# Gated linear attention on one core: the sixteen state steps of a half as one scan along the free axis

## The reference

```python
def step(S, inp):
    qt, kt, vt, gt = inp
    S = S * jnp.exp(gt)[..., None] + kt[..., None] * vt[..., None, :]
    ot = jnp.einsum('bhk,bhkv->bhv', qt, S)
    return (S, ot)
S0 = jnp.zeros((b, h, dk, dv), q.dtype)
_, o = jax.lax.scan(step, S0, (qT, kT, vT, gT))
...
g = jax.nn.log_sigmoid(x @ Wgk1 @ Wgk2 + bgk2) / GLN
```

## Time and profile before

| what | value |
|---|---|
| median of 3 runs | 3053.11 us (3050.43 to 3057.81) |
| span of the profiled execution | 3058.2 us, first to last instruction |
| first stage, of that span | about 676 us |
| PE busy, whole span | 2879.5 us (94%) |
| DVE busy, whole span | 2283.9 us (75%) |
| ACT busy, whole span | 1938.1 us (63%) |

### The profile page before, as it was taken

How to read it: one execution, slowest core, us unless ns; L and a number is a source line. 1 busy time by engine, 2 the same in 40 slices (tenths; PEclk the granted TensorE clock), 3 DMA queues, 4 the chain that set the end, 5 groups by cost and what they waited for, 6 DMA issues and landing times. The chain is left out here.

```text
span 3058.2 us, 63018 instructions
## 1 busy us (share of the span) xinstructions
PE 2879.5 (94%) x22889; PEld 1806.1 (59%) x22890; DVE 2283.9 (75%) x4031; ACT 1938.1 (63%) x3559; POOL 688.5 (23%) x965
## 2 busy tenths in 40 slices
PE   5999999986999999999999999999888999999998
PEld 4777777774333333333333333337777888888886
DVE  5777777764999999999999999967785454545443
ACT  3666666661888888888888888875543333333332
POOL 2222222222000000000000000001103555555554
PEclk7899999986999999999999999998889999999999
DMA  1223323223222222222222222217642333333332
GB/s 45 87 98 107 111 101 105 100 84 117 68 74 65 83 72 72 67 67 65 73 72 69 66 64 72 73 39 212 213 146 51 50 50 50 49 51 49 50 50 42
DMA packets 170745, 243.05 MB, mean 79 GB/s; under 512 B 30920, under 2 KB 118240, under 8 KB 170512
## 3 DMA queue, kind: packets, MB, share of 16 engines
q1 hardware_dynamic: 121920, 170.57, 18.4%
q0 software_dynamic: 31152, 52.33, 8.9%
q10 hardware_dynamic: 17440, 16.98, 1.7%
HBM read 126.53 MB, written 111.21 MB: 78 GB/s over the span
## 5 line engine op out<-in xcount | busy, mean ns | idle before, releaser
L1030 DVE TENSOR_REDUCE b_mxq<-b_p_m 128x1 f32<-128x1024 f32 x1024 | 1220.6, 1222 | 76.2 <-PE b_p_m L1057 67.2
L964 ACT ACTIVATE b_probs<-b_p_e 128x512 f32<-128x512 f32 x2048 | 1105.4, 597 | 140.7 <-PE b_p_e L1110 40.1
L1057 PE MATMUL b_p_m<-b_kst,b_qst 64*128 64x512 f32 x1536 | 568.2, 449 | 0.8 <-DVE b_mxq L1030 0.8
L1110 PE MATMUL b_p_e<-b_qst,b_kst 64*128 64x512 f32 x1536 | 559.6, 444 | 0.2 <-ACT b_probs L964 0.2
L1082 PE MATMUL b_p_o<-b_probs,b_vst 128*32 128x256 f32 x6160 | 481.9, 390 | 0.5 <-ACT b_probs L964 0.4
L1110 PEld LDWEIGHTS b_p_e<-b_qst,b_kst 64*128 64x128 f32 x1536 | 236.4, 184 | 312.3 <-ACT b_probs L964 266.0
L1849 ACT ACTIVATE d_act<-d_p_up 128x512 f32<-128x512 f32 x136 | 81.2, 597 | 490.7 <-PE d_p_up L1922 490.7
L1082 PEld LDWEIGHTS b_p_o<-b_probs,b_vst 128*32 128x32 f32 x6160 | 126.3, 108 | 243.4 <-issue 133.4
L1818 POOL DMA_INDIRECT out_dram<-d_y,d_to x136 | 217.7, 1601 | 216.8 <-DVE d_y L1883 204.1
L1937 PE MATMUL d_p_y<-w2T,d_hT 128*128 x1096 | 259.1, 379 | 0.8 <-ACT d_hT L1843 0.8
L1865 DVE TENSOR_SCALAR d_xh<-d_p_x,d_ln 128x128 fp32r<-128x128 f32 x272 | 82.9, 346 | 233.5 <-PE d_p_x L1916 233.5
(11 more groups left out here) (319 smaller groups left out, 4628.5 us busy)
## 6 DMA issues: line engine op xcount, KB each, us to landing
b_qst<-qk_d SPq DMA_DIRECT2D x288, 64.0 KB
b_kst<-qk_d SPq DMA_DIRECT2D x288, 64.0 KB
qk_d<-a_hi SPq DMA_DIRECT2D x32, 512.0 KB, 2.8
qk_d<-a_lo SPq DMA_DIRECT2D x32, 512.0 KB, 3.8
v_d<-a_v_s SPq DMA_DIRECT2D x16, 1024.0 KB, 4.5
o_d<-b_oT POOLq DMA_DIRECT2D x63, 256.0 KB, 2.7
b_vst<-v_d SPq DMA_DIRECT2D x48, 256.0 KB
raw<-in_L_ffn_w_dram SPq DMA_DIRECT2D x24, 512.0 KB, 4.9
```

Source lines behind the costliest of these rows:

```text
L964: nc.scalar.activation(probs[(2 * step + e % 4 // 2) % BUFS][:, (e % 2) * 512:(e % 2 + 1) * 512], p_e[(slot(e) if more1 else e) % EB][:], ...
L1030: V_.reduce_max(mxq[half][:, h, qt:qt + 1], p_m[j % 2][:], AX.X).then_inc(s["m_red"], 1)
L1057: mm(p_m[j % 2][:, kh * 512:(kh + 1) * 512], qst[r][rows(h), qt * P:(qt + 1) * P], kst[r][rows(h), kh * 512:(kh + 1) * 512], start=True, s ...
L1110: mm(p_e[u % EB][:], kst[r][rows(h), kt * P:(kt + 1) * P], qst[r][rows(h), a * 512:(a + 1) * 512], start=True, stop=True).then_inc(s["e_ps ...
```

## The change

The sixteen steps of DVE become one tensor_tensor_scan over 64 x 17 elements: `S` is laid out with the chunk as the innermost index (element v, c at 17 v + c), two new tiles of that shape hold the decays (`steps`, spread over the 64 values by ACT, with 0 at c = 0, which starts each of the 64 rows anew) and the increments (`added`, copied out of the four PSUM banks by ACT, bank by bank, with the carried state at c = 0). The copies into `Sbd` now read `S` with the value as the inner index, 17 elements (68 bytes) apart. PE signals the increments bank by bank, and its next input transposes wait for `added` and not for the last step. The mask tile, used once at the start, moves into `o2`.

```diff
-    S = sb("S", [P, NC + 1, DV])
+    S, steps, added = (sb(n, [P, DV, NC + 1]) for n in ("S", "steps", "added"))
...
+        def decay_steps(f):
...
+            act.wait_ge(s["exps"], f + 1)
+            A.copy(steps[:, :, 1:], decay[:].rearrange("p (o c) -> p o c", o=1).to_broadcast([P, DV, NC])).then_inc(s["steps_done"], 1)
+
+        def increments(f):
...
+            if f > 0:
+                act.wait_ge(s["S_done"], f)
+            for c in range(4):
+                act.wait_ge(s["inc_ps"], 4 * f + c + 1)
+                last = A.copy(added[:, :, 1:].rearrange("p v (t b) -> p b t v", b=4)[:, c], p_f[:, c, 0:T * DV].rearrange("p (t v) -> p t v", t=T))
+            last.then_inc(s["added_done"], 1)
...
-            act.wait_ge(s["S_step"], f * NC + 8 * part + 7)
+            act.wait_ge(s["S_done"], f + 1)
             for h in range(H):
-                last = A.copy(Sbd[h * DK:(h + 1) * DK, 8 * part:8 * part + 8, h * DV:(h + 1) * DV], S[h * DK:(h + 1) * DK, 8 * part:8 * part + 8, :])
+                last = A.copy(Sbd[h * DK:(h + 1) * DK, 8 * part:8 * part + 8, h * DV:(h + 1) * DV], S[h * DK:(h + 1) * DK, :, 8 * part:8 * part + 8].rearrange("p v c -> p c v"))
...
             keys(n + 1)
+            decay_steps(n + 1)
             attention_input(n)
+            increments(n + 1)
             rounded(n, 0)
...
+            if f % 2:
+                V_.tensor_copy(added[:, :, 0], S[:, :, NC]).then_inc(s["S_carry"], 1)
+            else:
+                V_.memset(added[:, :, 0], 0.0).then_inc(s["S_carry"], 1)
...
-            for c in range(NC):
...
-                V_.scalar_tensor_tensor(S[:, c + 1], S[:, c], decay[:, c:c + 1], p_f[:, c % 4, (c // 4) * DV:(c // 4 + 1) * DV],
-                                        ALU.mult, ALU.add).then_inc(s["S_step"], 1)
+            flat = [tile[:].rearrange("p v c -> p (v c)") for tile in (S, steps, added)]
+            V_.tensor_tensor_scan(flat[0], flat[1], flat[2], 0.0, ALU.mult, ALU.add).then_inc(s["S_done"], 1)
...
-                pe.wait_ge(s["S_step"], f * NC)
+                pe.wait_ge(s["added_done"], f)
```

More of the change, by code:

```diff
@@ L76, in gla_and_projections @@
     ident, ones = sb("ident", [P, P]), sb("ones", [P, P])
-    mask = sb("mask", [P, HT])
     maski = sb("maski", [P, HT], mybir.dt.int32)
@@ L94, in gla_and_projections @@
     AT = sb("AT", [P, H, HT])
-    S = sb("S", [P, NC + 1, DV])
+    S, steps, added = (sb(n, [P, DV, NC + 1]) for n in ("S", "steps", "added"))
     Sbd = sb("Sbd", [P, NC, D])
     o_s, o2 = sb("o_s", [P, T, D]), sb("o2", [P, T, D])
+    mask = o2[:].rearrange("p t d -> p (t d)")[:, 0:HT]
     ss, rs = sb("ss", [P, T * H]), sb("rs", [P, T * H])
@@ L116, in gla_and_projections @@
              "g0", "g1", "cum_done", "tail_done", "exps_rel", "exps_tail", "exps", "qtkt", "kh_done", "qh_done", "khT_ps", "khat_done",
-             "AT_ps", "AT_done", "inc_ps", "S_step", "S_carry", "Sbd_done", "o_ps", "o_s_done", "o2_done", "ss_done", "rs_eps", "rs_done", "on_done", "og_done",
+             "AT_ps", "AT_done", "inc_ps", "steps_done", "added_done", "S_done", "S_carry", "Sbd_done", "o_ps", "o_s_done", "o2_done", "ss_done", "rs_eps", "rs_done", "on_done", "og_done",
              "ogT_ps", "ogT_done", "wout_ps", "x1_done", "stb_done", "mvb_done", "roots_eps", "roots_done", "root0_done", "xr_done", "xrT_ps", "xrT_done", "xrTl_done",
@@ L255, in decays @@
             A.activation(decay[:], cum[:].rearrange("p (c j) -> p c j", j=C)[:, :, C - 1], ACT.Exp).then_inc(s["exps"], 1)
+        def decay_steps(f):
+            if not 0 <= f < N:
+                return
+            act.wait_ge(s["exps"], f + 1)
+            A.copy(steps[:, :, 1:], decay[:].rearrange("p (o c) -> p o c", o=1).to_broadcast([P, DV, NC])).then_inc(s["steps_done"], 1)
+        def increments(f):
+            if not 0 <= f < N:
+                return
+            if f > 0:
[4 more added lines that the diff above has]
+            last.then_inc(s["added_done"], 1)
         def keys(f):
@@ L322, in _ @@
         V_ = nc.vector
+        V_.memset(steps[:, :, 0], 0.0)
         V_.memset(ones[:], 1.0)
@@ L326, in _ @@
         V_.memset(keep[:].rearrange("p (c j) -> p c j", j=C)[:, :, 0:1], 0.0)
-        V_.tensor_copy(maski[:], mask[:]).then_inc(s["consts"], 1)
+        V_.tensor_copy(maski[:], mask).then_inc(s["consts"], 1)
         dve.wait_ge(s["consts"], 1)
@@ L455, in layer_norm, with carried @@
             V_.scalar_tensor_tensor(norm[:, h * T:(h + 1) * T, 1], mvb[:, :, 0], -1.0, roots[:, 0], ALU.mult, ALU.mult)
+        def carried(f):
+            if not 0 <= f < N:
+                return
+            if f > 0:
+                dve.wait_ge(s["S_done"], f)
+            if f % 2:
+                V_.tensor_copy(added[:, :, 0], S[:, :, NC]).then_inc(s["S_carry"], 1)
+            else:
+                V_.memset(added[:, :, 0], 0.0).then_inc(s["S_carry"], 1)
         def states(f):
@@ L459, in states @@
                 return
-            dve.wait_ge(s["inc_ps"], f + 1)
-            dve.wait_ge(s["exps"], f + 1)
+            dve.wait_ge(s["S_carry"], f + 1)
+            dve.wait_ge(s["steps_done"], f + 1)
+            dve.wait_ge(s["added_done"], f + 1)
             if f > 0:
                 dve.wait_ge(s["Sbd_done"], 2 * f)
[L464 to L468, removed]
-            for c in range(NC):
[L470 to L473, removed]
-                V_.scalar_tensor_tensor(S[:, c + 1], S[:, c], decay[:, c:c + 1], p_f[:, c % 4, (c // 4) * DV:(c // 4 + 1) * DV],
-                                        ALU.mult, ALU.add).then_inc(s["S_step"], 1)
+            flat = [tile[:].rearrange("p v c -> p (v c)") for tile in (S, steps, added)]
+            V_.tensor_tensor_scan(flat[0], flat[1], flat[2], 0.0, ALU.mult, ALU.add).then_inc(s["S_done"], 1)
         def rests(h, parts):
@@ L518, in _ @@
             layer_norm(n)
+            carried(n + 1)
             states(n + 1)
@@ L526, in _ @@
         g.memset(mhalf[:], -0.5)
-        g.memset(mask[:], 1.0).then_inc(s["zero"], 1)
+        g.memset(mask, 1.0).then_inc(s["zero"], 1)
         pool.wait_ge(s["zero"], 1)
         g.affine_select(out=ident[:], in_=ident[:], compare_op=ALU.not_equal, fill=1.0, base=0, pattern=[[-1, P]], channel_multiplier=1)
-        m4 = mask[:].rearrange("p (t c j) -> p t c j", c=4, j=C)
+        m4 = mask.rearrange("p (t c j) -> p t c j", c=4, j=C)
         g.affine_select(out=m4, in_=m4, compare_op=ALU.is_ge, fill=0.0, base=0, pattern=[[0, T], [-C, 4], [0, C]], channel_multiplier=1).then_inc(s["zero"], 1)
@@ L687, in increments @@
                                   V[rows, t, h * DV:(h + 1) * DV], start=True, stop=True)
-            last.then_inc(s["inc_ps"], 1)
+                last.then_inc(s["inc_ps"], 1)
         def outputs(h, tiles):
```

## The result

The changed kernel takes 3120.39 us (median of 4 runs, 3119.49 to 3122.14), the kernel before beside it 3055.46 us (4 runs). The ratio is 1.0213, with a 95% interval of 1.0199 to 1.0227: about 65 us slower. The forecast was 3097, its range 3073 to 3150.

A forecast was written before the change was run, and what follows sets the result against it. PE was taken to bound the first stage's bodies, with ACT's eight copies into `Sbd` the chain with little slack. 15 bodies x 2.9 us gave 43.5, so 3053.1 + 43.5 = 3097 us; range 3073 to 3150.

The forecast's parts named there:

- PE bounds the body, DVE's time is not on the path: First stage's bodies: PE waits for neither the steps nor the `rests`, so DVE's saved 2.6 us a body gain nothing.
- The scan at 2.43 us, ACT's new copies inside its idle time: Scan 2.43 us for 5.03; `decay_steps` 1.02 us and `increments` 370 to 590 ns each, hidden in ACT's idle time.
- The rival of dear writes: ACT's jumping `increments` writes make the scan late, from about 0.9 us a copy; at 1.2 us, 3114 us; chance 0.04.
- The copies into `Sbd` pay for the jump: ACT's eight copies read 68 bytes apart at 0.83 ns an element extra: 616 to about 1040 ns each; chance 0.58.
- The slack of 0.5 us and no one behind to absorb the rest: At the outputs, 3.40 us more copying less about 0.5 us slack leaves PE waiting 2.9 us a body, nothing absorbing it.
- a second fall: Rival: new PE gaps make the granted clock fall again in each body, 3147 us, or 3122 in half; chance 0.27.
- a sign of being wrong: The prediction called itself wrong if, among other signs, the granted clock fell inside the outputs.
- The first half: Earlier transposes there, `Sbd`'s first part ending about when PE comes; put at 0, within 1.4 us either way.

The follow-up runs named there:

- The scan with plain copies: Changed kernel, but DVE lays the states out chunk by chunk so ACT's eight copies into `Sbd` read neighbours; 3056.58 us, 1.0001 of the kernel before.
- the two exchanges of layout: Changed kernel with ACT's copies reading neighbours again: 3056.58 us; kernel before with only the layout of `S` changed: 3121.96 us.
- the copies of 128 x 256: Kernel before plus four copies in ACT's idle time, inner steps 2, 4, 8, 17 elements; jumping in reading 3053.86 us, in writing 3059.55 us.
- one more plain copy a part: Kernel before with one extra plain 32 x 512 ACT copy ahead of each group of four copies into `Sbd`; 3067.82 us, ratio 1.0040.
- steps kept, jump put on: Kernel before with its sixteen steps, only the layout of `S` changed to that of the changed kernel; 3121.96 us, ratio 1.0208.
- jump in the writing: Changed kernel with the eight copies' index order swapped: they read eight neighbours at a time and write 1024 bytes apart; 3127.4 us, ratio 1.0243.
- three more plain copies: Kernel before with three extra plain 32 x 512 ACT copies ahead of each group of four copies into `Sbd`; 3115.71 us, ratio 1.0193.

## Why the prediction was right, and where its size was off

**PE bounds the body, DVE's time is not on the path.** Right. The scan with plain copies measures 1.0001 of the kernel before.

**The scan at 2.43 us, ACT's new copies inside its idle time.** Right: 2.42 us. The increments took 624 ns each and not 370 to 590, the spread decays 1.07 us; the states were still there 1.75 us before ACT came. The rival of dear writes had the price in part, but it stayed under its turning point of 0.9 us a copy. That point was itself set too low: by the prediction's own times the copies start at 342.57, so four of them and the scan's 2.43 us are done by 349.74 up to about 1.2 us a copy, where the rival counted a loss of 1.1 us a body.

**The copies into `Sbd` pay for the jump.** Right in the mechanism, as the two exchanges of layout show from both sides. The size was taken too low. I took 0.83 ns an element, between readings of 0.69 and 0.94; measured is (1095 - 616) / 512 = 0.94, the upper bound, the one that came from the medians. That it was met so closely is luck: the bound rests on 15 ns in one instruction, and the copies of 128 x 256 put the price between 0.74 and 0.94. With it the working gave 3.35 us a body, and the body measures 3.41. This term was thus worth 51 us and not 43.5.

**The slack of 0.5 us and no one behind to absorb the rest.** Right in the main: one more plain copy a part made most bodies 0.6 us longer where the slack makes it 0.75, and three more cost nearly what the change costs (ratio 1.0193 against 1.0213).

**The clock.** The forecast left it as it is and gave a second fall 0.27 as a rival. It fell a second time in four of fifteen bodies, in or behind the outputs' second wait, which the prediction had named as a sign of being wrong; the four pairs of bodies cost 13 us beyond the 3.41 a body. The forecast and this rival thus each hold part of the truth: 3120 lies above the forecast's own 3088 to 3103, and inside the stated range only by the room that was left for this rival. The falls go with the gaps. Between 100 and 665 us the kernel before and the scan with plain copies, which have no such gap, show no second fall; the four kernels with gaps of 1.5 to 1.8 us show three (the changed kernel), four (steps kept, jump put on), one (jump in the writing) and four (three more plain copies). The same gaps stand in the other bodies without a fall. What decides it in a given body stays open; no experiment here separates it.

**The first half.** Put at 0, measured 0.6 us later.

Together: 51 + 13 + 0.6 is 65 us for the measured 65. The 13 is the rest that 15 times 3.41 leaves, and it goes to the clock because it lies in the bodies with a second fall. Against the forecast's 43.5, the reading price accounts for 8 us and the clock for 13.

## What to carry to other kernels

A layout that suits one engine's instruction is paid for by whoever reads it next: here 2.6 us a body were saved on an engine that nobody waited for, and 3.8 us laid on the one whose copies had 0.5 us to spare. Before a layout is turned, list every reader with the inner step that it gets, and price a step of 16 bytes or more, for fp32 in SBUF, as about a second pass over each element on ACT, in reading and in writing. A small instruction that already jumps (16 elements, 11 to 15 ns too many) was enough to find that price ahead, to within its spread. Once an engine's slack is used up, count also what new gaps on PE may do to its clock: here they took a fifth of the loss.

## What the runs showed of the hardware

ACT paid 0.7 to 0.9 ns an element more for an inner step of 16 bytes or more on fp32 in SBUF, reading or writing: for 32 x 512 and 616 ns plain, 1095 ns with reads 68 bytes apart and 1080 with writes 1024 bytes apart; for 128 x 256 and 0.45 us at 8 bytes, 0.64 to 0.69 us at 16, 32 and 68 bytes, with no rise from 16 to 68. DVE laid out 128 x 512 with the same 68-byte reads in 626 ns, and its steps of 128 x 64, jumping in one SBUF input and in the output, went only from 281 to 331 ns. A wait of PE for ACT can stand in the trace as "issue" (35.6 us in 22 waits): it is found by setting the end of ACT's part beside PE's next start. The granted clock fell a second time in some bodies with two gaps of 1.5 to 1.8 us in the outputs, and between 100 and 665 us in none without them.
